# Low rank of a feed-forward block as array tiles: column-tiled f32 partial sums and 32-row products

## What is computed

```
h = take(table, ids)
h = h + recurrence(layernorm(h), Wf, Wi, Wh)
x = layernorm(h)
z = x @ (tern(w_fc) * s_fc).T + gate * (x @ v.T @ fast_b.T @ u.T)     # 256 -> 1024, rank 16
r = maximum(z, 0)
out = h + (r * r) @ (tern(w_proj) * s_pj).T                              # 1024 -> 256
```

## Time and profile before

| | |
|---|---|
| median of 3 executions | 933.69 us (933.27 to 934.51) |
| the profiled execution's own time | 933.25 us |
| its span, first to last instruction | 931.4 us |
| busy in the span | TensorE 893.2, ScalarE 781.3, VectorE 745.0, GpSimd 462.6 us |
| mean granted TensorE clock | 0.992 of full speed |

### The profile page before, as it was taken

One profiled execution on the slowest core, in us unless ns is written; L12 is line 12 of the kernel. 1 busy time (PEld: TensorE's weight loads), 2 busy tenths in 40 slices (PEclk: granted clock), 3 DMA queues, 4 the chain that ended last, 5 costly groups with the idle time before them and its releaser, 6 DMA issues.

```text
span 931.4 us, 17427 instructions
## 1 busy us (share of the span) xinstructions
PE 893.2 (96%) x5169; PEld 511.4 (55%) x5169; DVE 745.0 (80%) x1309; ACT 781.3 (84%) x1159; POOL 462.6 (50%) x457
## 2 busy tenths in 40 slices
PE   3889999999999999999999999999999999999976
PEld 2335555555555555555555555655555555555544
DVE  6799888878888878888887788888888888877663
ACT  4578998888898888889888889988888998888765
POOL 6545554556655455664545566554556555522110
PEclk9989999999999999999999999999999999999989
DMA  4223344342333333233333323323332332343220
GB/s 143 46 50 62 94 67 91 97 91 61 82 83 78 85 96 87 58 87 79 78 90 95 79 65 85 81 73 96 96 74 69 84 83 73 96 91 70 64 71 24
DMA packets 229579, 73.91 MB, mean 79 GB/s; under 512 B 204342, under 2 KB 224384, under 8 KB 229552
## 3 DMA queue, kind: packets, MB, share of 16 engines
q1 hardware_dynamic: 223408, 69.38, 31.3%
q0 software_dynamic: 6144, 4.21, 2.0%
HBM read 27.68 MB, written 24.64 MB: 56 GB/s over the span
## 4 chain that ended last, share of the span: by engine, by line
PE 91%; ACT 3%; DVE 2%; issue 2%; POOL 1%; DMA 1%; SPq 0%; ACTq 0%; POOLq 0%; DVEq 0%
PE bank L762 35%; PE y_ps L719 23%; PE bank L801 23%; PE bank L805 6%; PE bank L702 3%; PE turned L730 2%; ACT normed L476 1%; ACT relu L528 1%; ACT sq L541 1%; DMA w_raw<-wh 0%; POOL rows_raw L379 0%; DMA x_cols<-x_rows 0%; DVE stats L877 0%; POOL rstd L394 0%; DVE y_sb L1064 0%
## 5 line engine op out<-in xcount | busy, mean ns | idle before, releaser
L801 PE MATMUL bank<-x_cols,fc_t 128*128 128x512 f16 x1024 | 265.4, 382 | 0.0
L389 POOL TENSOR_SCALAR var_eps<-moments 128x4 f32<-128x4 f32 x64 | 59.7, 933 | 355.1 <-DVE moments L881 355.0
L762 PE MATMUL bank<-x_cols,w_hi 128*128 128x512 f16 x768 | 229.8, 381 | 4.6 <-ACT cand_lin L517 3.0
L762 PE MATMUL bank<-x_cols,w_lo 128*128 128x512 f16 x768 | 229.4, 380 | 0.0
L719 PE MATMUL y_ps<-proj_t,sq_hi 128*128 128x256 bf16 x1024 | 225.6, 273 | 2.1 <-DVE sq_lo L1056 2.0
L719 PE MATMUL y_ps<-proj_t,sq_lo 128*128 128x256 bf16 x1024 | 225.6, 273 | 0.0
L379 POOL DMA_INDIRECT rows_raw<-table,idx_now x128 | 161.3, 1260 | 60.2 <-issue 31.0
L528 ACT ACTIVATE relu<-bank,relu_scale 128x512 f32<-128x512 f32 x256 | 165.2, 688 | 13.0 <-PE bank L805 13.0
L801 PEld LDWEIGHTS bank<-x_cols,fc_t 128*128 128x128 bf16 x1024 | 100.9, 99 | 115.4 <-issue 3.2
L1056 DVE TENSOR_TENSOR sq_lo<-sq,sq_hi 128x1024 f16<-128x1024 f32 x128 | 150.4, 1214 | 15.0 <-ACT sq L541 15.0
L476 ACT ACTIVATE normed<-h,shift,rstd 128x256 f32<-128x256 f32 x256 | 132.9, 605 | 8.7 <-POOL shift L397 8.7
(11 more groups left out here) (129 smaller groups left out, 929.0 us busy)
## 6 DMA issues: line engine op xcount, KB each, us to landing
out<-out_sb SPq DMA_DIRECT2D x32, 512.0 KB, 2.9
spill<-hid_blocks SPq DMA_DIRECT2D x30, 256.0 KB
hid_rows<-spill SPq DMA_DIRECT2D x120, 64.0 KB
rows_raw<-table,idx_now POOLq DMA_INDIRECT x128, 2.8
x_cols<-x_rows SPq DMA_TRANSPOSE x124
sq<-w_fc SPq DMA_DIRECT2D x1, 1024.0 KB
pj_raw<-w_proj SPq DMA_DIRECT2D x1, 1024.0 KB
w_raw<-wf SPq DMA_DIRECT2D x1, 256.0 KB
```

What stands on the lines that cost most here:

```text
L762: ins = pe.matmul(bank[gate_bank[p]][:, :], w[:, k, q, :], x_part(0, par, part)[:, :, k, :], start=(k == 0 and w is w_hi and part == 0), s ...
L801: pe.matmul(dst[:, :], fc_t[:, f, k, :], x_part(1, 0, part)[:, :, k, :], start=(k == 0 and part == 0), stop=False)
```

## The change

The low rank of chunk m is made in three stages. `low_parts`: each of the four products (two halves of the 256 features, high and low input) now has a stationary of 32 columns (16 ranks high, 16 low) and goes to its own 32 rows of one PSUM bank (`low_ps`, the upper half of `turned`), as tiles of the array side by side. ScalarE copies the bank as f32 (`copy_parts`). `low_sums`: one f32 matmul with the 0/1 matrix `spread` (a one wherever two indices agree modulo 16) sums the partial sums and repeats the result in all 128 rows. Then `low_high` and `low_low` split it into f16 high and low parts on all 128 rows, and `narrow` adds the term to four blocks at a time: each matmul uses 32 rows of `low_u` and of the high or the low part, at another quarter of the rows for each of the four blocks.

The order on the queues changes too. TensorE: `low_parts` after gate 3, gates 4 and 5, `low_sums`, the fc_t matmuls of blocks 0 and 1 (`wide`), `narrow(0, 2)`, which closes blocks 0 and 1 and opens 2 and 3, `wide` 2 to 5, the transposes, `narrow(4, 2)`, `wide` 6 and 7. ScalarE: `copy_parts` between forget and inp of the second half, `low_high` behind cand_lin. VectorE: `low_low` behind `candidate(1)`. The banks of gates and blocks rotate by the step's parity. In steps 1, 2 and 32 the order is: `low_parts`, `wide` 0 and 1, `low_sums`, `wide` 2 and 3, `narrow(0, 4)`, `wide` 4 and 5, `narrow(4, 2)`, `wide` 6 and 7.

```diff
-        low_a = sb("low_a", [P, KD, P], F16)
+        low_a = sb("low_a", [P, KD, 2, R], F16)
+        spread = sb("spread", [P, P])
-        low = sb("low", [P, CHUNK], F16)
+        parts = sb("parts", [P, CHUNK])
+        low_hi = sb("low_hi", [P, CHUNK], F16)
+        low_lo = sb("low_lo", [P, CHUNK], F16)
-        gate_bank = (0, 1, 2, 3, 1, 2)
-        fc_bank = (3, 0, 1, 2, 3, 0, 1, 2)
+        low_ps = turned[:, CHUNK:2 * CHUNK]
+        turned_half = turned[:, 0:CHUNK].rearrange("p (j d) -> p j d", j=TILES)
...
+        def gate_bank(p, par):
+            return bank[(p + 2 * par) % 4]
+        def fc_bank(f, par):
+            return bank[(f + 2 + 2 * par) % 4]
...
+            def copy_parts(m):
+                act.wait_ge(part_done, m + 1)
+                wait(act, low_done, m)
+                act.activation(parts[:, :], low_ps, ACT.Copy).then_inc(parts_ready, 1)
             def low_high(m):
                 act.wait_ge(low_done, m + 1)
                 wait(act, fc_done, FC * m)
-                act.activation(low[:, :], bank[0][:, :], ACT.Copy).then_inc(low_hi_ready, 1)
+                act.activation(low_hi[:, :], low_ps, ACT.Copy).then_inc(low_hi_ready, 1)
...
-                    evict(n, 1, 0, forget, ACT.Sigmoid)
-                    evict(n, 1, 1, inp, ACT.Sigmoid)
+                    evict(n, par, 1, 0, forget, ACT.Sigmoid)
+                copy_parts(m)
+                if front:
+                    evict(n, par, 1, 1, inp, ACT.Sigmoid)
+                    evict(n, par, 1, 2, cand_sig, ACT.Sigmoid)
+                    evict(n, par, 1, 3, cand_lin, ACT.Identity, 0.5)
                 low_high(m)
-                if front:
-                    evict(n, 1, 2, cand_sig, ACT.Sigmoid)
-                    evict(n, 1, 3, cand_lin, ACT.Identity, 0.5)
                 back(n)
...
                 for k in range(KD):
                     for part in range(2):
-                        ins = pe.matmul(bank[0][:, :], low_a[:, k, :], x_part(1, 0, part)[:, :, k, :],
-                                        start=(k == 0 and part == 0), stop=(k == KD - 1 and part == 1))
-                ins.then_inc(low_done, 1)
+                        at = slice(BLOCK * (2 * k + part), BLOCK * (2 * k + part + 1))
+                        ins = pe.matmul(low_ps[at, :], low_a[:, k, :, :].rearrange("p a r -> p (a r)"),
+                                        x_part(1, 0, part)[:, :, k, :], start=True, stop=True)
+                ins.then_inc(part_done, 1)
+            def low_sums(m):
+                pe.wait_ge(parts_ready, m + 1)
+                pe.matmul(low_ps, spread[:, :], parts[:, :], start=True, stop=True).then_inc(low_done, 1)
...
+                def free(f):
+                    if f > 3:
+                        pe.wait_ge(relu_ready, FC * m + f - 3)
+                    elif front:
+                        pe.wait_ge(gate_taken, 8 * n + (2, 5, 6, 8)[f])
+                    else:
+                        pe.wait_ge(relu_ready, FC * (n - 2) + (7, 8, 5, 6)[f])
+                def narrow(first_f, opened):
+                    for f in range(first_f + opened, first_f + 4):
+                        free(f)
+                    for part, ready in ((low_hi, low_hi_ready), (low_lo, low_lo_ready)):
+                        pe.wait_ge(ready, m + 1)
+                        for i in range(4):
+                            f, at = first_f + i, slice(BLOCK * i, BLOCK * (i + 1))
+                            ins = pe.matmul(fc_bank(f, par)[:, :], low_u[at, f * P:(f + 1) * P], part[at, :],
+                                            start=(part is low_hi and i >= opened),
+                                            stop=(part is low_lo and i < opened))
+                            if part is low_lo and i < opened:
+                                ins.then_inc(fc_done, 1)
...
+                if steady and front:
+                    narrow(0, 2)
+                    wide(2, False)
+                    wide(3, False)
+                else:
+                    low_sums(m)
+                    wide(2, True)
+                    wide(3, True)
+                    narrow(0, 4)
+                wide(4, True)
+                wide(5, True)
+                if front and not first:
+                    turn_upper(n)
+                narrow(4, 2)
+                wide(6, False)
...
-                low_half()
                 if ahead:
                     x_low(0, n + 1)
                 if front:
                     candidate(1)
+                low_low()
+                if front:
                     weigh(1)
                     scan(1)
```

More of the change, by code:

```diff
@@ L598, in step @@
                     scale_fc(1)
-                    evict(1, 1, 2, cand_sig, ACT.Sigmoid)
-                    evict(1, 1, 3, cand_lin, ACT.Identity, 0.5)
+                    copy_parts(0)
+                    evict(1, par, 1, 2, cand_sig, ACT.Sigmoid)
+                    evict(1, par, 1, 3, cand_lin, ACT.Identity, 0.5)
                     low_high(0)
@@ L736, in step @@
                 front = known_below(n, N)
-                back = not isinstance(n, int) or n > 0
                 start = isinstance(n, int) and n == 0
@@ L741, in step, with gate @@
                 steady = not isinstance(n, int) or n > 2
-                n_late = second or steady
+                def gate(p):
+                    e, g = divmod(p, 3)
+                    if p < 4:
+                        wait(pe, relu_ready, FC * (n - 2) + 5 + p)
+                        if first:
+                            pe.wait_ge(gate_taken, 8)
+                    else:
+                        pe.wait_ge(gate_taken, 8 * n + (4, 4 if start else 3)[p - 4])
+                    q = 2 * g + e
+                    for k in range(KD):
+                        for w in (w_hi, w_lo):
+                            for part in range(2):
+                                ins = pe.matmul(gate_bank(p, par)[:, :], w[:, k, q, :], x_part(0, par, part)[:, :, k, :],
+                                                start=(k == 0 and w is w_hi and part == 0),
+                                                stop=(k == KD - 1 and w is w_lo and part == 1))
+                    ins.then_inc(gate_done, 1)
@@ new lines, in free, with wide @@
+                def free(f):
[5 more added lines that the diff above has]
+                        pe.wait_ge(relu_ready, FC * (n - 2) + (7, 8, 5, 6)[f])
+                def wide(f, opens):
+                    if opens:
+                        free(f)
+                    if first:
+                        pe.wait_ge(fc_landed[f // 4], 16)
+                    for k in range(KD):
+                        for part in range(2):
+                            ins = pe.matmul(fc_bank(f, par)[:, :], fc_t[:, f, k, :], x_part(1, 0, part)[:, :, k, :],
+                                            start=(opens and k == 0 and part == 0),
+                                            stop=(not opens and k == KD - 1 and part == 1))
+                    if not opens:
+                        ins.then_inc(fc_done, 1)
```

198 lines of the change are left out of this document (91 added, 107 removed).

## The result

| | before | after |
|---|---|---|
| median (runs of one chip, beside each other) | 933.61 us (933.27 to 934.51) | 983.54 us (982.99 to 986.3) |
| ratio | | 1.0539, 95% interval 1.0518 to 1.056 |
| span of the profiled execution | 931.4 us | 982.0 us |

A forecast was written before the change was run, and what follows sets the result against it. TensorE's list of work was taken to bound the 27.28 us step. 933.25 + 26.7 (29 steps at 0.92: 0.32 list, 0.60 waits) + 6.2 for the ends gave 966 us, range 945 to 1000.

The forecast's parts named there:

- The f32 sum: One f32 matmul of 512 columns per step on TensorE, summing the partial products: 0.86 us, up to 1.6 at face value.
- A quad, q: TensorE's time for four tiled matmuls, five such groups a step: 0.35 us each, taken between 0.216 and 0.51.
- A change, d: TensorE's cost at each of six changes a step between whole-array and tiled work: 0.05 us.
- The rival of a full drain: Each change between whole-array and tiled work drains TensorE, 0.166 us: 1.39 more a step, 980 us; chance 22%.
- The clip wait: TensorE waits before narrow(4, 2) for ScalarE's clip 3, queued behind pair 0's squares: 0.65 us a step.
- The condition 1.05 - q - d: Length of TensorE's wait for clip 3 at narrow(4, 2), from a quad's time q and a change's d: 0.65 us.
- The first low quad: After the last gate slot, TensorE arrives at 2.99 us, low_low's result at 2.94: no wait unless q + d is below 0.35.
- No wait above q of 0.26: Parts quad ahead of gate 4 finds x_cols ready for q above 0.26; at 0.216 a margin of only 0.04 us.
- The period: Steady step as 24.01 + 3q + 3d + max(2.94, 2.59 + q + d): 28.20 us against 27.28.
- The start: Steps 1 and 2, with another order: step 1 some 3.4 us longer, off by 2 either way; step 2 0.7.
- The tail: Last step: clip 1 at 912.5 instead of 910.38, ScalarE's chain after it as before: 2.1 us.
- ScalarE's chain to the end is unchanged: In the tail, from clip 1 on, ScalarE's work takes as long as before, so only clip 1's 2.1 us delay counts.

The follow-up runs named there:

- experiment 4: Changed kernel with all low_u matmuls of a quad on the same 32 rows, one quarter of the array: 1036.07 us, 1.1107 of the kernel before.
- experiment 5: Changed kernel with the moves of Experiment 1 and experiment 2 (943.01 us), plus the f32 transposes between the second low_u pair's high and low quads: 951.46 us.
- Experiment 1: Also `e1_order`: changed kernel with ScalarE's clips 2 and 3 ahead of pair 0's two squares: 951.01 us, 1.0192 of the kernel before.
- experiment 7: Experiment 6's kernel with the partial sums as an f16 pair, summed by two f16 matmuls instead of one f32, and copy_parts ahead of inp: 938.55 us.
- experiment 2: Changed kernel with the parts quad behind gate 4 on TensorE and copy_parts behind inp on ScalarE: 969.54 us, 1.0385 of the kernel before.
- Experiment 6: Also `e5_start`: moves of Experiment 1 and experiment 2, plus, in step 1, low_low behind scan(0) and low_high behind x_high(0, 2): 940.38 us.
- e8_low_first: Experiment 7's kernel with low_high ahead of cand_lin on ScalarE and low_low ahead of candidate(1) on VectorE: 932.76 us, 0.9996 of the kernel before.

## Why the prediction was right, and where it fell short

The direction and its reason held: TensorE's own line gains nothing, and a wait for the clips comes on top. The sum, 966.15, was 17.7 below the profiled execution's 983.85: an x_cols wait that I had costed at nothing was there (14.5), the start and the tail were sized too small (4.7, of it 1.0 spread between executions, and 3.0), changes and the chain to clip 3 cost more than I gave them (4.4 and 4.9), and a quad that was cheaper than I took it paid back 13.6. So the number came out nearer than its terms: some 31 us too little on one side and 14 too much on the other, and that they partly cancel is luck.

- **The f32 sum.** Forecast 0.86, not the up to 1.6 that the earlier trace rows would allow at face value; measured 0.86 (442.46 to 443.32). The price per column of the transposes carried over. That the row lies at half pace fits this, but what halves it isn't shown: the granted clock reads 1.00 there (9.00 to 11.00 us, kernel before).
- **A quad, q.** Forecast 0.35 between 0.216 and 0.51; measured 0.22 to 0.23 (experiment 4 has 0.87 with no parallel work). Taking the middle was wrong: the 0.51 had the four weight loads of a quad one after another, at 0.098 each, and they take 0.10 together. (The Trainium skill's 3.07 times, "TensorE: Matmul & The Clock Gate", Part 3, gave q as 0.28 by the estimate in the prediction; the trace goes further than that, 3.8 times.)
- **A change, d.** Forecast 0.05 from a change of type, which measures nothing here either; measured 0.09 to 0.12 (experiment 5). The type was the wrong neighbour: what costs is the change between whole-array and tiled matmuls. The rival of a full drain, 0.166, had the place of the cost right and its size somewhat high, and its 980 lies near the measured 983.5 for other reasons: at d = 0.166 and the measured q its sum would be 24.01 + 0.66 + 0.50 + 2.98 = 28.15, or about 965.
- **The clip wait.** Forecast 0.65 with 4.93 for the chain from first low quad to clip 3; measured 0.72 in the bracket and 5.10 for the chain (445.37 to 450.47). The 0.17 is mostly in its first link: clip 0 started 0.55 behind the low quad, not 0.42, which I had read off whole-array matmuls; the other 0.05 is its last, from the end of clip 3 to TensorE (0.10 for 0.05). Experiment 1 shows that the order of ScalarE's queue makes this wait. The condition 1.05 - q - d held too: in experiment 4, with q at 0.87, about 0.1 of the wait is left.
- **The first low quad.** Forecast that TensorE arrives last, at 2.94 to 2.99; measured 2.91 (442.46 to 445.37) with no bracket. Right, and experiment 7 shows how thin it was: TensorE 0.43 earlier there waited.
- **"No wait above q of 0.26" for x_cols.** This is the step that failed. I took 5.29 from x_rows to the parts quad out of the tail of the kernel before. In the changed kernel's loop it is 5.67 (433.00, where ScalarE starts x_rows, to 438.67), and 6.25 in another step. With q at 0.22 there was no margin left, 0.04 of a wait by the prediction's own count, so that most of what the transfer is longer shows up as a wait: 0.50 a step by experiment 2, 14.5 us. The loop itself is not the reason for the first 0.3 to 0.4: the changed kernel's own tail, with no gather beside it, has 5.66 (946.78 to 952.44), and the tails of the ten variants have 5.59 to 5.66. What makes them longer than the 5.29 before is not shown.
- **The period.** With what was measured: 24.01 + 3 x 0.22 + 3 x 0.10 + 2.91 + 0.17 of the longer chain = 28.05, and experiment 2, which has the clip wait alone, runs at 28.05. Plus 0.50 for x_cols it is 28.55, and 27.28 + 1.27 is 28.55. So the sum's form was right and the terms that were off are q (3 x 0.13 too long, and 0.08 in the last term, 0.47 in all), d (0.15 too short), the chain (0.17) and the missing 0.50.
- **The start.** Forecast 4.1, measured 8.8. Its parts quad starts 1.0 late (58.33 for 57.35 in the earlier trace rows); in the ten variants it starts at 57.05 to 57.90, on both sides of the kernel before, so this 1.0 is spread between executions and not a cost of the change, and "nothing" for the prologue's edits stands. Step 1 is the term that was too small, 3.4 forecast: step 2's first gate starts 8.2 late (79.83 for 71.61), so step 1 cost 7.2. I had costed its low parts as a chain and not asked who is queued behind them. VectorE stood 6.11 at `low_low` with `candidate(0)`, the output scales that the clips need, and the scan behind it; `relu_scale` came at 69.84 instead of 63.04. Experiment 6 gives 1.9 of this back and the clip order of experiment 1 another 2.4, counted from the parts quad.
- **The tail.** Forecast 2.1, measured 5.1. From step 32's low_a to the end it is 29.6 (952.44 to 982.0) for 26.8, so 2.8: the second clip starts 7.6 behind low_a for 5.8 before (1.8), and "ScalarE's chain to the end is unchanged" failed by 0.9, because clip 4 now waits for a quad that itself waits for clip 3. The other 2.3 lie ahead of it, between step 31's projection and step 32's low_a: step 31's own clip wait and x_cols wait, which the forecast had put into the 29 steps, and 0.4 of x_cols in the tail itself.

What stays open: the brackets for x_cols are about 0.2 in one step and 0.6 to 1.1 in the next through most of the loop, and steps are about 28.3 and 28.9 by turns. The trace has a lead. GpSimd's first gather of new rows and TensorE's parts quad of a long step, and the gather of the next, short one, changed kernel:

```profile
405.26 2.15 POOL L394 DMA_INDIRECT rows_raw<-table,idx_now  x1 [0.89 <-POOL idx_now L385]
410.31 0.40 PE L728 MATMUL turned<-x_cols,low_a 128*32 128x512 f16 x4 [0.82 <-DMA x_cols<-x_rows]
...
436.25 1.59 POOL L394 DMA_INDIRECT rows_raw<-table,idx_now  x1 [0.89 <-POOL idx_now L385]
```

In the long step the gather starts with SP's issue of the transfer (405.22), in the short one 2.1 behind it (434.15). So it is in every step from 238 to 839 us: gather with the issue, 6.04 to 6.49 from x_rows to the quad; gather later, 5.60 to 5.66, also where three short steps follow each other. In `e1_order` the gather comes later in every step, and the alternation is gone. No run moved the gather alone, and one step that is written out (parts quad at 896.47) waits 1.5 with no gather at all, so this is not shown to be the cause, and not the only one.

## What to carry to other kernels

When an engine's line is full, cost a new chain beside it from the moment that its last input leaves the engine to the moment that its result is wanted, and then read which work of no hurry stands ahead of each link in the other queues: three such reorderings gave back 3.3%, 0.6% and 0.5% here, and moving the first link behind more of TensorE's own work 1.4%, while making TensorE's own work cheaper gained 0.2% until the queues beside it were put in order. A cover of a few hundredths of a microsecond is none: here 0.3 to 1.2 more in the transfer than the one row that I had went straight through it. And where tiles of the array take turns with whole-array matmuls, put the tiled ones together, since each change costs and shows only as a distance between starts.

## What the runs showed of the hardware

Four matmuls of 32 rows and 512 columns on four quarters of the array took 0.22 to 0.23 us, as long as one whole-array matmul of 512 columns, and 0.87 on one quarter. Going from whole-array to tiled matmuls or back cost 0.09 to 0.12 each time, and 0.16 once (experiment 5), booked as busy. ("TensorEngine Tiling (Array Packing)", Key Properties, in the Trainium skill has the engine drain when the tiling mode changes; the trace agrees that there is a gap at each such change, at or somewhat under the 0.166 by which two matmuls of 512 columns overlap, and none where only the type changes.)

One idle stretch cost more than its length. In the profiled execution of `e8_low_first` TensorE once waited 1.96 us for a clip, and the windows behind it, that kernel, show the granted clock at 0.50, the level of 1.2 GHz, for some three microseconds, and at 1.00 again after that:

```profile
160.49 0.60 PE L801 MATMUL bank<-x_cols,w_hi 128*128 128x512 f16 x2 [1.96 <-ACT relu L552]
```
```profile
161.10:164.50 3.40, 3.40 (x9) 1.18 (x8) 3.25 (x8) 3.40 (x4) 2.80 (x3) 0.50 0.00 0
165.20:168.20 3.00, 3.00 (x19) 1.74 (x18) 2.00 (x3) 2.89 (x6) 2.81 (x3) 1.00 0.01 3
```

Nine matmuls in the 3.4 us at the lower level against 19 in the 3.0 at the full one; the step took 30.68 for 27.04, so 1.96 of waiting cost about 3.7. A wait of this length need not do it: in `e5_start` TensorE waited 1.87 (ended at 81.78), and the clock reads 1.00 behind it. The changed kernel's waits between 120 and 915 us, up to 1.5 long, were never followed by such a stretch: the clock stands at 1.00 there.
